# Moving a copy of the logits, the sums of the exponentials and the ranks' copy from VectorE to ScalarE in a mixture-of-experts feed-forward kernel

## What is computed

```python
def cond_layer(v, q):
    x = (n * v + v.sum(1)) * relu(q @ W3 + b3)[:, None, :]
    return relu(x @ W2 + b2)

h = cond_layer(x, cond)                    # 8192 tokens x 512
scores = softmax(h @ gate_w.T)             # 64 experts
topk_w, topk_i = top_k(scores, 6)
# each expert takes its first 64 tokens in the order of tokens (capacity 64)
y_e = (silu(h_e @ w_gate[e]) * (h_e @ w_up[e])) @ w_down[e]
y = sum over the 6 experts of a token of weight * y_e
shared = (silu(h @ sw_gate) * (h @ sw_up)) @ sw_down
out = x + y + shared
```

## Time and profile before

| | |
|---|---|
| median of 3 runs | 1278.72 us (1278.03 to 1279.66) |
| the profiled execution | 1280.25 us, of which the span of its instructions 1278.4 us |
| TensorE busy | 1254.0 us, 98% of the span |
| VectorE busy | 708.5 us, 55% |
| ScalarE busy | 338.0 us, 26% |
| mean granted TensorE clock | 0.995 |

### The profile page before, as it was taken

How to read it: one execution, slowest core, us unless ns; L and a number is a source line. 1 busy time by engine, 2 the same in 40 slices (tenths; PEclk the granted TensorE clock), 3 DMA queues, 4 the chain that set the end, 5 groups by cost and what they waited for, 6 DMA issues and landing times.

```text
span 1278.4 us, 16131 instructions
## 1 busy us (share of the span) xinstructions
PE 1254.0 (98%) x6152; PEld 934.8 (73%) x6152; DVE 708.5 (55%) x1536; ACT 338.0 (26%) x550; POOL 144.1 (11%) x118
## 2 busy tenths in 40 slices
PE   5899999999999999999999999999999999999998
PEld 5687888888888888888867666666666666666666
DVE  6688888978888787886823233232232323323322
ACT  3444332332334333233212111121111201211110
POOL 0000000000000000000001222121222222212220
PEclk8899999999999999999999999999999999999999
DMA  7814417053441615325757989969979989898952
GB/s 199 254 38 134 138 48 220 9 177 91 128 144 38 194 41 182 91 86 132 280 196 278 284 266 294 318 236 283 326 220 330 308 246 291 283 300 267 294 127 77
DMA packets 129277, 250.92 MB, mean 196 GB/s; under 512 B 21296, under 2 KB 59312, under 8 KB 127024
## 3 DMA queue, kind: packets, MB, share of 16 engines
q1 hardware_dynamic: 117712, 224.71, 52.1%
q0 software_dynamic: 11488, 25.17, 9.8%
HBM read 197.14 MB, written 61.10 MB: 202 GB/s over the span
## 4 chain that ended last, share of the span: by engine, by line
PE 92%; DVE 3%; SPq 3%; DMA 1%; ACT 1%; issue 1%; ACTq 0%; DVEq 0%
PE bank L1213 22%; PE bank L1215 21%; PE bank L1214 21%; PE bank L1446 12%; PE bank L1469 7%; SPq L459 2%; PE bank L1230 2%; PE bank L1428 1%; PE bank L1336 1%; PE bank L1335 1%; PE bank L1271 1%; PE bank L1274 1%; PE bank L1455 1%; DMA hT<-h 1%; PE bank L1284 0%
## 5 line engine op out<-in xcount | busy, mean ns | idle before, releaser
L1213 PE MATMUL bank<-hh,gu 128*128 128x512 f32 x704 | 281.3, 400 | 0.1
L1215 PE MATMUL bank<-hh,gu 128*128 128x512 f32 x704 | 274.7, 390 | 0.0
L1214 PE MATMUL bank<-hl,gu 128*128 128x512 f32 x704 | 274.3, 390 | 0.0
L1213 PEld LDWEIGHTS bank<-hh,gu 128*128 128x128 f32 x704 | 132.5, 188 | 38.7 <-issue 12.8
L863 DVE TENSOR_TENSOR prod<-bank,prod 128x512 f32<-128x512 f32 x96 | 66.1, 689 | 165.8 <-PE bank L1215 144.0
L1215 PEld LDWEIGHTS bank<-hh,gu 128*128 128x128 f32 x704 | 132.1, 188 | 28.6
L1214 PEld LDWEIGHTS bank<-hl,gu 128*128 128x128 f32 x704 | 132.4, 188 | 25.3
L616 ACT ACTIVATE ah<-prod 128x512 fp32r<-128x512 f32 x96 | 60.6, 632 | 260.8 <-DVE prod L863 260.8
L1213 PE MATMUL bank<-sdh,ah 128*128 128x512 f32 x320 | 126.8, 396 | 0.0
L1214 PE MATMUL bank<-sdl,ah 128*128 128x512 f32 x320 | 124.6, 390 | 0.0
L1215 PE MATMUL bank<-sdh,al 128*128 128x512 f32 x320 | 124.6, 389 | 0.0
(11 more groups left out here) (117 smaller groups left out, 1604.9 us busy)
## 6 DMA issues: line engine op xcount, KB each, us to landing
wg<-in_L_ffn_w_gate_dram SPq DMA_DIRECT2D x64, 704.0 KB
wu<-in_L_ffn_w_up_dram SPq DMA_DIRECT2D x64, 704.0 KB
wd<-in_L_ffn_w_down_dram SPq DMA_DIRECT2D x64, 512.0 KB
table<-hrow SPq DMA_DIRECT2D x64, 256.0 KB, 4.3
x<-in_x_dram SPq DMA_DIRECT2D x15, 1024.0 KB, 8.4
wd<-in_L_ffn_w_down_dram SPq DMA_DIRECT2D x64, 192.0 KB
out_dram<-outst SPq DMA_DIRECT2D x36, 256.0 KB, 2.7
hT<-h SPq DMA_DIRECT2D x8, 1024.0 KB, 3.9
```

The source lines that it names most:

```text
L1213: nc.tensor.matmul(o, st_h, mv_h, start=first_mm, stop=False)
L1214: nc.tensor.matmul(o, st_h, mv_l, start=False, stop=False)
L1215: return nc.tensor.matmul(o, st_l, mv_h, start=False, stop=last_mm)
```

## The change

Three pieces of work move from VectorE to ScalarE, with two new semaphores, `llow_ready` and `cand_ready`.

1. The copy of the logits' low part to `lg` becomes `take_low(n)` on ScalarE. `route(n)` waits for it (`llow_ready`) where it waited for the transposed logits. In passes 1 to 7 `take_low(a)` stands behind `take_cond(b, 0)`, and `take_low(b)` behind `silu(v, 0)`. In pass 0 `take_low(a)` stands behind `take_lraw(b)` and `take_low(b)` behind `silu(v, 3)`.
2. The sum of the exponentials leaves `score(n)`. `exp_scores(n)` becomes four `Exp` of 128x64, each with an accumulated sum (`accum_out`). In passes 1 to 7 `exp_scores(a)` moves from behind `take_cond(b, 0)` to behind `take_cond(b, 1)`.
3. The copy of the transposed ranks becomes `take_ranks(i)` on ScalarE. The first merge round waits for it (`cand_ready`), and so does TensorE's next `ranksT`. A pass counts 16 merge steps in place of 17.

```diff
-        MERGE_STEPS = 1 + 2 * NR
+        MERGE_STEPS = 2 * NR
...
+            def take_low(n):
+
+                act.wait_ge(s.logits_filled, n + 1)
+                wait(act, s.z_ready, n)
+                parts = logits_bank(n)[:, :].rearrange("p (j h e) -> p h j e", j=J, h=2)
+                copy(lg[:, :, :], parts[:, 1, :, :]).then_inc(s.llow_ready, 1)
+
+            def take_ranks(i):
+                act.wait_ge(s.ranksT_filled, i + 1)
+                wait(act, s.merge_step, MERGE_STEPS * i)
+                copy(cand[:, CAP:CAP + CH], bank[7][:, :]).then_inc(s.cand_ready, 1)
+
             def exp_scores(n):
                 act.wait_ge(s.z_ready, n + 1)
                 wait(act, s.scores_ready, n)
-                nc.scalar.activation(ez[:, :, :], z[:, :, :], ACT.Exp).then_inc(s.exp_ready, 1)
+                for j in range(J):
+                    op = nc.scalar.activation(ez[:, j, :], z[:, j, :], ACT.Exp, accum_out=ssum[:, j:j + 1])
+                op.then_inc(s.exp_ready, 1)
...
                     elif oc == 0:
+                        take_low(a)
+                    elif oc == 1:
                         exp_scores(a)
                 take_lraw(b)
+                if i == 0:
+                    take_low(a)
                 if more:
                     split_xm(c, 0)
                 silu(v, 0)
+                if i > 0:
+                    take_low(b)
                 if more:
                     split_xm(c, 1)
                 split_a(v, 0)
+                if not more:
+                    take_ranks(i)
...
                 split_a(v, 2)
+                if 1 < i < ND - 1:
+                    take_ranks(i)
                 silu(v, 3)
                 if i == 0:
+                    take_low(b)
                     split_piece(7)
+                if i == 1:
+                    take_ranks(i)
...
             def route(n):
 
                 parts = logits_bank(n)[:, :].rearrange("p (j h e) -> p h j e", j=J, h=2)
-                dve.wait_ge(s.logits_filled, n + 1)
-                link(nc.vector.tensor_copy(lg[:, :, :], parts[:, 1, :, :]))
+                dve.wait_ge(s.llow_ready, n + 1)
                 link(nc.vector.tensor_tensor(lg[:, :, :], parts[:, 0, :, :], lg[:, :, :], ALU.add))
...
             def score(n):
                 dve.wait_ge(s.exp_ready, n + 1)
-                link(nc.vector.reduce_sum(ssum[:, :], ez[:, :, :], AX))
...
-            def take_ranksT(i):
-                dve.wait_ge(s.ranksT_filled, i + 1)
-                wait(dve, s.merge_step, MERGE_STEPS * i)
-                nc.vector.tensor_copy(cand[:, CAP:CAP + CH], bank[7][:, :]).then_inc(s.merge_step, 1)
...
             def ranksT(i):
                 pe.wait_ge(s.ranks_ready, 2 * i + 2)
-                wait(pe, s.merge_step, MERGE_STEPS * (i - 1) + 1 if i > 0 else 0)
+                wait(pe, s.cand_ready, i)
```

More of the change, by code:

```diff
@@ L223, in adaln_moe_ffn_kernel @@
             logits_filled = sem("logits_filled")
+            llow_ready = sem("llow_ready")
             route_step = sem("route_step")
@@ L229, in adaln_moe_ffn_kernel @@
             ranksT_filled = sem("ranksT_filled")
+            cand_ready = sem("cand_ready")
             merge_step = sem("merge_step")
@@ L928, in score @@
                                         ALU.mult).then_inc(s.scores_ready, 1)
-            def take_ranksT(i):
-                dve.wait_ge(s.ranksT_filled, i + 1)
-                wait(dve, s.merge_step, MERGE_STEPS * i)
-                nc.vector.tensor_copy(cand[:, CAP:CAP + CH], bank[7][:, :]).then_inc(s.merge_step, 1)
             def merge(i, r):
                 eight = first[:, 8 * r:8 * r + 8]
+                if r == 0:
+                    dve.wait_ge(s.cand_ready, i + 1)
+                wait(dve, s.merge_step, MERGE_STEPS * i + 2 * r)
+                nc.vector.max(eight, cand[:, :]).then_inc(s.merge_step, 1)
                 dve.wait_ge(s.merge_step, MERGE_STEPS * i + 1 + 2 * r)
-                nc.vector.max(eight, cand[:, :]).then_inc(s.merge_step, 1)
-                dve.wait_ge(s.merge_step, MERGE_STEPS * i + 2 + 2 * r)
                 if r < NR - 1:
@@ L1016, in body @@
                         merges(0, (5, 6))
-                    else:
-                        take_ranksT(i)
                     split_a(v, 2)
```

## The result

The changed kernel takes 1282.92 us as a median of 11 runs (1281.65 to 1285.79), the kernel before 1279.66 us in the same comparison (11 runs, 1274.93 to 1280.77). The ratio of the two is 1.0033, with a 95% interval of 1.0024 to 1.0043: slower by some 4.2 us (3.1 to 5.5) by the ratio; the two medians lie 3.26 us apart. The forecast was +3.84 us, 1282.6.

A forecast was written before the change was run, and what follows sets the result against it. TensorE, busy 1099.5 of 1099.5 us from 150.5 us on, was taken as the bound, so only its waits count. 1.99 (pass 1) + 1.66 (pass 2) + 0.19 (pass 0) = 3.84 us over 1278.72: 1282.6, range 1280.7 to 1285.6.

The forecast's parts named there:

- the forecast's limit: TensorE's waits in pass 0 (1.84 us) and pass 1 (0.28): no more than 2.1 us can be won, under 0.2%.
- Pass 1, +1.99 us: `route(b)` waits for `take_low(b)` behind `silu(v, 0)`, so `product(v, 0)` and TensorE's tile 4 come 1.99 us later.
- Pass 2, +1.66 us: Same late `take_low(b)`: VectorE's add again 1.99 us late, tile 4 at 227.67 against 226.01, +1.66 us.
- Passes 3 to 7, nothing: Passes 3 to 6: add 0.94 us late, covered by 2.6 us slack before tile 4; pass 7 waits for TensorE anyway.
- Pass 0, +0.19 us: Chain ending TensorE's 1.84 us wait for `take_cond(c, 0)`: four `Exp` for one, against VectorE's relief, net +0.19 us.
- X: Time of the four `Exp` in pass 0, where one took 0.32 us: 0.64 to 1.76, taken as 1.40 us.
- a readout of 0.09 and no overlap: Middle assumption for each `Exp` with its sum in pass 0, giving X = 1.40 us.
- The relief of 0.89: Pass 0, VectorE: sum in `score(a)` (0.44 us with hand-over) and low copy in `route(b)` (0.45) gone, 0.89 us earlier.
- The clock, 0.05: Rival: pass 1's 2.3 us wait lowers TensorE's clock, twelve matmuls slow, 2.5 us more, 1285.1 us; chance 0.05.
- The dear readout: Rival: each sum's readout takes 0.5 us, X is 3.0, in all +7.6 us, 1286.3 us; chance 0.07.
- the passes with no slack: Rival: the 2.6 us slack in passes 3 to 6 goes too, four more stalls, +6.6 us, 1289.2; chance 0.03.
- the copy that would be there in time: Rival: `take_low(b)` ends before VectorE needs it; pass 0 gains up to 0.57 us, pass 1 0.28, 1277.9; chance 0.07.

The follow-up runs named there:

- the last experiment: Low copy ahead of `split_xm(c, 0)` in passes 1 to 7, pass 0's `exp_scores(b)` behind `take_cond(c, 1)`, against the kernel with only the former: 1276.29 us.
- the pair of runs with one wait each: Changed kernel with `take_low(b)` ahead of `split_xm(c, 0)` in pass 2 only (1282.84 us), or in passes 1 to 7 except pass 2 (1281.27 us).
- low copy only: Against the kernel before, only the low copy moves to ScalarE; sums and ranks' copy stay on VectorE, `exp_scores(a)` placed as in the change: 1283.83 us, ratio 1.0037.
- early in pass 2 only: Against the changed kernel, `take_low(b)` stands ahead of `split_xm(c, 0)` in pass 2 only: 1282.84 us in one run.
- the changed kernel's second profile: The changed kernel run once more, nothing altered: 1280.91 us in one run.
- the early copy: Against the changed kernel, `take_low(b)` moves ahead of `split_xm(c, 0)` on ScalarE in passes 1 to 7: 1276.68 us, ratio 0.9985 to the kernel before.

## Why the prediction was right

**The bound.** TensorE was full before and is full after but for named waits; from pass 2's ranks to the end the profiles agree within 0.1 us (1046.95 and 1047.00), so no work saved on VectorE there counted. But the forecast's limit, that no more than 1.84 + 0.28 = 2.1 us can be won, was too low: the last experiment won 2.6. It took the idle time in a row's bracket as the whole price of a wait. Around the wait of 99.13 us in the earlier trace rows the kernel before has

```profile
96.91 0.39 PE L1215 MATMUL bank<-xmh,w2l 128*128 128x512 f32 x1
...
99.47 0.40 PE L1214 MATMUL bank<-xml,w2h 128*128 128x512 f32 x1
```

From start to start that is 2.22 us less the usual 0.23, so 1.99 lost and not 1.84, and the first matmul behind the wait holds the next back by 0.34 instead of 0.23: 2.10 in all. Pass 1 lost 0.28 + 0.11 = 0.39 in the same way. Together that is 2.5 us.

**Pass 1, +1.99 us.** Measured +1.94 in the execution whose clock held. The wait shown as 2.10 us is 148.93 - 146.44 - 0.23 = 2.26 from start to start, where the forecast had 2.3. The copy out of PSUM took the 0.38 us of the condT row, the start 0.50 behind `silu`'s was 0.49.

**Pass 2, +1.66 us.** Measured +1.77 to +1.79. The start of tile 4 came 228.12 - 226.27 - 0.23 = 1.62 us late, near the forecast's 1.66, which left out the 0.11 that the first matmul behind a wait costs in addition. That pass 1's wait does not pay for pass 2's is shown by the pair of runs with one wait each.

**Passes 3 to 7, nothing.** As forecast: from ranks to ranks 75.83 or 75.84 in each of passes 3 to 6, and 65.81 against 65.82 in pass 7, with VectorE waiting 2.34 us in pass 3.

**Pass 0, +0.19 us.** This term was mis-sized: it came out at -0.32. X was taken as 1.40 us with no overlap, between 0.64 and 1.76; it is 0.97. The step that failed is "a readout of 0.09 and no overlap", for which no row spoke. The readout exists, but the instructions overlap on both sides. The relief of 0.89 was right: with 0.65 for the exponentials 0.24 is left, and the stretch gave 0.3.

**The clock, 0.05.** This rival was priced too high, 2.5 against 1.54 us, and given far too small a chance. I took "2.3 lies nearer to the first" as a reason; there was only no row between 1.84 and 4.27. The price counted twelve slow matmuls, as at 47.83 us, and it was eight. The clock fell in three of the four profiles that have pass 1's wait of 2.10 us (the changed kernel, low copy only, early in pass 2 only, but not the changed kernel's second profile), and behind the one of 2.17 us.

**Sum.** Without the clock, by the second profile of the changed kernel, -0.29 + 1.94 + 1.79 = 3.4 us; with it, 5.0. The measured 4.2 (3.1 to 5.5) lies between. That the forecast's 3.84 lies so near is partly luck: pass 0 came out 0.5 us lower than forecast, and the clock, which the sum left out, adds 1.5 us in some executions. The two waits, 3.65 us of the sum, were right in place, cause and size. The dear readout, the passes with no slack, and the copy that would be there in time did not come; the last is what the early copy makes true by hand, and its 0.75 us by the stretches is near the 0.85 (0.57 + 0.28) of that rival.

**One `Exp` of 64 columns.** By the formula of the Trainium skill, ScalarE: Activation LUTs, section "What ACT_TABLE_LOAD costs", an `Exp` of 64 columns takes 186 + 53 = 239 ns as an estimate; the rows have 243 ns as the mean of 64. The estimate of 0.68 us for X that the forecast drew from it took the sums as free, and counted three overlaps where the four `Exp` and `take_cond` behind them have four; what measured 0.97 has four readouts in it, of 187 ns each in these rows before their overlap.

## What to carry to other kernels

When work moves to an idle engine, its place in that engine's order counts more than its length: a copy of 0.38 us behind a table load and an activation cost TensorE 1.94 + 1.79 = 3.7 us in two passes, and more where its clock fell, while the same copy some places sooner in the order cost nothing. Before moving it, look at what stands ahead of it there, at what those instructions wait for, and which tile of the bounding engine is released from behind the receiver. And on a run that one engine bounds, the waits of that engine say how little can be won, if they are counted from start to start (here 2.5 us behind the start, where the brackets gave 2.1); the better version came from shortening the chain that ends its one wait, by moving a table load out of it.

## What the hardware showed that I had not expected

A wait of TensorE of 2.10 us was followed by the lower clock in one execution of the same kernel and not in another: a granted clock of 0.51, the level of 1.2 GHz, from 149 to 152 us in the one, and 1.00, the level of 2.4 GHz, with 0.23 us from matmul to matmul in the other. Behind 60 us, waits of 0.87 to 1.86 us in these profiles were never followed by it, and one of 2.08 in pass 0 neither; the one of 2.17 and, from 45 us on, each of 2.91 to 5.56 us was. After the wait of 3.24 us at the start of the kernel with the low copy early, two matmuls still ran at full speed before it fell (the next starts are 45.63, 45.87 and 46.27):

```profile
45.30 0.50 PE L1236 MATMUL bank<-xmh,w2h 128*128 128x512 f32 x1 [3.24 <-ACT h L635]
```

And an accumulated sum on ScalarE is an instruction of its own of 187 ns (64 in the run), of which some 0.1 us remain when they stand in a row (an estimate: 0.97 / 4 = 0.24 from `Exp` to `Exp`, less the 0.14 that an `Exp` of 0.243 us with an overlap of 0.10 would take).
